# Four small reorderings around the end of the neighbour search in a four-layer graph kernel

## The reference

```python
z = _lap_mul(A, x) @ W1 + b1
z = jax.nn.leaky_relu(z, negative_slope=0.1)
d2 = sq[:, None] + sq[None, :] - 2.0 * (z @ z.T)
S = jnp.exp(-jnp.sqrt(jnp.maximum(d2, 0.0) + 1e-10) / 2.0)
S = jnp.where(ranks < 4, S, 0.0)          # the four nearest rows of each row
A2 = S + A
out = _lap_mul(A2, x) @ W2 + b2           # d * (A2 @ (d * x)), d from the row sums of A2
x = _layernorm(x + out)
...
h_N = jnp.matmul(adj, x)                  # fourth layer
out = jnp.maximum(concat([x, h_N]) @ W.T + b, 0.0)
```

## Time and profile before

| | us |
|---|---|
| median of three runs | 1466.86 |
| profiled execution, first to last instruction (span) | 1463.7 |
| PE busy | 1393.7 (95%) |
| DVE busy | 836.0 (57%) |
| ACT busy | 451.0 (31%) |
| POOL busy | 246.9 (17%) |

### The profile page before, as it was taken

One profiled execution on the slowest core, in us unless ns is written; L12 is line 12 of the kernel. 1 busy time (PEld: TensorE's weight loads), 2 busy tenths in 40 slices (PEclk: granted clock), 3 DMA queues, 4 the chain that ended last, 5 costly groups with the idle time before them and its releaser, 6 DMA issues.

```text
span 1463.7 us, 20350 instructions
## 1 busy us (share of the span) xinstructions
PE 1393.7 (95%) x7300; PEld 737.9 (50%) x7300; DVE 836.0 (57%) x1311; ACT 451.0 (31%) x979; POOL 246.9 (17%) x358
## 2 busy tenths in 40 slices
PE   6999999999999799999999987999999889999997
PEld 4776676666444354444544532444444344444454
DVE  6877766665224423323322269999999356555044
ACT  4776665665100000000000045666666200000011
POOL 2111110111100100000000000111111277774000
PEclk9999999999999999999999999999999989999999
DMA  9999998897998979788778520004443799999962
GB/s 311 400 383 389 365 331 300 325 318 266 359 382 331 379 308 346 306 316 328 298 292 310 227 72 1 15 17 137 134 130 115 242 370 401 380 386 394 352 234 71
DMA packets 112814, 403.26 MB, mean 276 GB/s; under 512 B 10368, under 2 KB 28384, under 8 KB 91232
## 3 DMA queue, kind: packets, MB, share of 16 engines
q1 hardware_dynamic: 72672, 314.33, 57.8%
q0 software_dynamic: 20576, 77.07, 14.0%
q10 hardware_dynamic: 19488, 10.80, 2.4%
HBM read 337.67 MB, written 64.49 MB: 275 GB/s over the span
## 4 chain that ended last, share of the span: by engine, by line
PE 70%; DVE 10%; DMA 10%; issue 7%; ACT 2%; POOL 0%; ACTq 0%; SPq 0%; DVEq 0%; POOLq 0%
PE acc L1137 10%; PE acc L1138 9%; PE acc L1139 9%; PE pt L1201 4%; DMA at_scratch<-region 3%; PE pt L1277 3%; PE pt L1278 3%; PE pt L1279 3%; DVE hT L1021 3%; PE pt L1137 3%; PE pt L1139 3%; PE pt L1138 3%; DMA region<-in_adj 3%; PE acc L1186 2%; PE acc L1182 2%
## 5 line engine op out<-in xcount | busy, mean ns | idle before, releaser
L1137 PE MATMUL acc<-region,yop 128*128 128x512 f16 x681 | 259.6, 381 | 16.6 <-DMA region<-at_scratch 16.6
L1201 PE MATMUL pt<-ident,region 128*128 128x128 f32 x1024 | 243.1, 277 | 18.8 <-DMA region<-in_adj 9.6
L1138 PE MATMUL acc<-region,yop 128*128 128x512 f16 x681 | 259.5, 381 | 0.0
L1139 PE MATMUL acc<-region,yop 128*128 128x512 f16 x681 | 259.5, 381 | 0.0
L969 DVE SCALAR_TENSOR_TENSOR region<-pt,region 128x512 f16<-128x512 f32 x200 | 135.3, 686 | 76.9 <-ACT region L631 76.4
L1201 PEld LDWEIGHTS pt<-ident,region 128*128 128x128 f32 x1024 | 145.9, 143 | 61.2 <-issue 16.1
L677 ACT ACTIVATE region<-pt 128x512 f32<-128x512 f32 x256 | 132.8, 602 | 109.4 <-PE pt L1284 95.8
L631 ACT ACTIVATE region<-pt 128x512 f16<-128x512 f32 x200 | 117.8, 596 | 108.6 <-PE pt L1201 94.0
L1021 DVE MAX8 hT<-region 128x8 f32<-128x4096 f32 x32 | 141.2, 4411 | 2.4 <-ACT region L677 2.4
L1137 PEld LDWEIGHTS acc<-region,yop 128*128 128x128 f16 x681 | 66.7, 98 | 98.7 <-issue 14.6
L598 ACT ACTIVATE std<-mv,eps_ln 128x4 f32<-128x4 f32 x32 | 9.5, 297 | 334.5 <-DVE mv L803 334.5
(11 more groups left out here) (235 smaller groups left out, 2157.8 us busy)
## 6 DMA issues: line engine op xcount, KB each, us to landing
region<-at_scratch SPq DMA_DIRECT2D x166, 1280.0 KB, 7.8
region<-in_adj SPq DMA_DIRECT2D x64, 1024.0 KB, 8.9
at_scratch<-region POOLq DMA_DIRECT2D x40, 768.0 KB, 7.0
at_scratch<-region POOLq DMA_DIRECT2D x40, 512.0 KB, 7.6
region<-at_scratch SPq DMA_DIRECT2D x76, 256.0 KB, 2.7
x_scratch<-xout ACTq DMA_DIRECT2D x16, 256.0 KB, 12.3
gath_all<-x_scratch POOLq DMA_DIRECT2D x12, 256.0 KB, 4.1
xin<-at_scratch SPq DMA_DIRECT2D x12, 256.0 KB, 2.8
```

Of the source, the lines that this page charges most:

```text
L1137: nc.tensor.matmul(into, y[:, 0, kt, :], high, start=(kt == first_tile), stop=False)
L1138: nc.tensor.matmul(into, y[:, 0, kt, :], low, start=False, stop=False)
L1139: return nc.tensor.matmul(into, y[:, 1, kt, :], high, start=False, stop=(kt == last_tile))
L1201: ins = nc.tensor.transpose(pt[kt % 4][:, t * P:(t + 1) * P], nat[u % 4][:, t, (kt % TPC) * P:(kt % TPC + 1) * P], ident[:, :])
```

## The change

Four things are moved; no arithmetic is added or removed.

1. PE: kept columns of chunks 4 and 5 no longer stand together ahead of row 24. The order is row 24, kept of chunk 4, projection of x2 of group 6, row 25, kept of chunk 5, turn of group 7, row 26, projection of group 7, rows 27 to 31.
2. POOL: the four residual loads are issued ahead of the small steps of group 7, behind the store of y of group 6.
3. ACT issues the late units 0, 1, 2 and 3; SP keeps the rest. Unit 0 waits for the search of row 30, units 1 and 2 for the search of row 31, unit 3 for y and its store.
4. The slot order of late units becomes 4, 3, 2, 1, 0 (it was 4, 3, 2, 0, 1).

```diff
-LATE_ORDER = [4, 3, 2, 0, 1]
+LATE_ORDER = [4, 3, 2, 1, 0]
-WIDE_REST = [24, 25, 26, 27, 28, 29, 30, 31]
-LATE_AT = {29: 0, 30: 1, 31: 2}
+ACT_LATE = 4
@@ sync
-                if kt in LATE_AT:
-                    sp.wait_ge(near_used, KT - 1 if LATE_AT[kt] == 0 else KT)
-                    load_late(LATE_AT[kt])
             sp.wait_ge(acc_full, nth(ALL, 4, WIDE - 1))
-            sp.wait_ge(yop_ready, nth(YOP, "y", NCH - 1))
-            sp.wait_ge(xT_full, nth(XT, 4, NCH - 1))
-            for b in range(2):
-                sp.wait_ge(y_stored[b], 16 * NCH // 2)
-            for k in range(len(LATE_AT), len(LATE)):
-                load_late(k)
+            for k in range(ACT_LATE, len(LATE)):
+                load_late(sp, k)
@@ gpsimd
+            def load_res():
+                pool.wait_ge(near_full, KT * NCH)
+                for t in range(TPC):
+                    pool.dma_start(res_rows(t // 2, 0, NCH)[:, :, t % 2, :], x2_rows[:, t, :, :]).then_inc(res_loaded, 16)
             for g in range(NCH):
+                if g == NCH - 1:
+                    load_res()
                 for stage_of in (distances, degree_sums, scales, low_y):
@@ scalar
             for i in range(KT + TPC + 1):
+                if i == KT:
+                    act.wait_ge(near_used, KT - 1)
+                    load_late(act, 0)
+                if i == KT + 1:
+                    act.wait_ge(near_used, KT)
+                    load_late(act, 1)
+                    load_late(act, 2)
...
+            act.wait_ge(yop_ready, nth(YOP, "y", NCH - 1))
+            act.wait_ge(xT_full, nth(XT, 4, NCH - 1))
+            for b in range(2):
+                act.wait_ge(y_stored[b], 16 * NCH // 2)
+            load_late(act, ACT_LATE - 1)
@@ tensor
+            wide_products(24)
+            kept_narrow(NARROW_KEPT[0])
+            pe.wait_ge(near_copied, copies(KT - 1, NCH - 1))
+            pe_project_x2(pe, NCH - 2)
+            wide_products(25)
+            kept_narrow(NARROW_KEPT[1])
+            pe_turn(pe, 4, NCH - 1)
+            wide_products(26)
+            pe_project_x2(pe, NCH - 1)
+            for kt in range(27, KT):
+                wide_products(kt)
```

More of the change, by code:

```diff
@@ L339, in load_x0, with load_late @@
             eng.dma_start(x0[:, part, :], x.rearrange("(t p) f -> p t f", p=P)[:, part, :]).then_inc(x0_loaded[q], 16)
+        def load_late(eng, k):
+            p, c, u = LATE[k]
+            slot = LATE_SLOTS[k]
+            if slot in LATE_SLOTS[:k]:
+                eng.wait_ge(*late_released(max(b for b in range(k) if LATE_SLOTS[b] == slot)))
+            eng.dma_start(ring[slot].rearrange("p k h n -> p (k h n)"), at_dram[c, u, :, :]
+                          ).then_inc(late_loaded_unit[slot], 16)
         block = ctx.enter_context(nc.Block())
@@ L406, in _ @@
             sp.wait_ge(acc_full, 4 * NCH)
[L407 to L413, removed]
             for kt in range(KEPT, KT):
@@ L537, in low_y @@
                                         ).then_inc(yop_ready, 1)
+            x2_rows = x_dram[2].rearrange("(c t p) f -> p t c f", p=P, t=TPC)
+            def load_res():
+                pool.wait_ge(near_full, KT * NCH)
+                for t in range(TPC):
+                    pool.dma_start(res_rows(t // 2, 0, NCH)[:, :, t % 2, :], x2_rows[:, t, :, :]).then_inc(res_loaded, 16)
             for g in range(NCH):
+                if g == NCH - 1:
+                    load_res()
                 for stage_of in (distances, degree_sums, scales, low_y):
@@ L547, in _ @@
                     load_x2(g + 2)
[L550 to L553, removed]
             pool.wait_ge(near_used, KT)
@@ L1377, in chunk_columns, with kept_narrow @@
                 return last
-            for c in NARROW_KEPT:
+            def kept_narrow(c):
                 pe.wait_ge(near_copied, copies(KT - 1, c))
                 chunk_columns(4, c, range(KEPT))
-                pe.wait_ge(near_copied, copies(KT - 1, NCH - 1))
-                if c == NARROW_KEPT[0]:
-                    pe_project_x2(pe, NCH - 2)
-                else:
-                    pe_turn(pe, 4, NCH - 1)
-            for kt in WIDE_REST:
+            wide_products(24)
[8 more added lines that the diff above has]
+            for kt in range(27, KT):
                 wide_products(kt)
-                if kt == WIDE_REST[1]:
-                    pe_project_x2(pe, NCH - 1)
             pe.wait_ge(near_copied, KT * NCH)
```

## The result

| | before | changed |
|---|---|---|
| median of four runs | 1466.98 us (1465.03 to 1467.61) | 1475.32 us (1474.55 to 1481.33) |
| ratio | | 1.0054, 95% interval 1.0033 to 1.0076 |
| span of the profiled execution | 1463.7 us | 1472.6 us |

The forecast was 1469.6 us, with a range of 1461 to 1474. The time fell outside it, on the slow side. A ratio of 1.0054 is 7.9 us; the interval goes from 4.8 to 11.2, so the change is clearly slower, if by little.

A forecast was written before the change was run, and what follows sets the result against it. The prediction took the chain from GpSimd's small steps through the gathers to VectorE's residuals as the limit. PE's projection of chunk 4 moves 1213.3 - 1210.56 = +2.7 us; 1463.7 + 2.7 + 3.2 = 1469.6 us, range 1461 to 1474.

The forecast's parts named there:

- the hold of the fourth load: On GpSimd, the fourth residual load waits for the three ahead, starting at 1162.4; distances start 16.7 us later.
- PE's wait for xT: Before the projection of group 7, PE, done with row 26 by 1153.5, waits for xT until 1168.
- end of the wide stage: PE finishes rows 28 to 31 at 1184 (1179 to 1187), against 1186.92 before.
- a wait of 4.0 for residual(0): At the projection of chunk 1, PE arrives at 1190.7 and waits 4 us for VectorE, until 1194.7.
- 1.7 for the clock: Between the projections of chunks 1 and 4, PE loses 1.7 us (0 to 2.3) at half clock after idling.
- 3.1 for the units: Two early ScalarE units, 2.62 MB, delay GpSimd's fourth load by 3.1 us, out of 0 to 7.4.
- a queue shares and doesn't block: On the DMA engines, GpSimd's and SyncE's queues took 61% and 41% when both had work.
- The units pass the loads: Rival, DMA engines from 1148: third load lands at 1166.3, gathers 1179.6; about +6 us, 1472.8; chance 15%.
- Held only until the first has landed: Rival, GpSimd's queue: the fourth load waits only for the first; gathers at 1168.5; -4.3 us, 1462.6; chance 21%.
- no hold: Rival, GpSimd's queue: the fourth load isn't held; distances at 1149.5, gathers at 1165.6; about -7 us, 1460; chance 11%.
- Faster by the whole 19 us: Rival, PE's rows 28 to 31: PE wins all 19 us; needs residual(0) by 1175; called excluded, no chance given.
- nothing gained, nothing lost: Late units issued by ScalarE: all but the last come earlier, with no gain or loss by itself.

The follow-up runs named there:

- e4: Changed kernel with late units issued by SyncE between tiles of rows 29 to 31 again (parts 3 and 4 undone): 1469.76 us, ratio 1.0006.
- e7: Changed kernel with PE's projection of group 7 moved behind row 27: 1476.27 us, ratio 1.0044 to the kernel before.
- e1: Changed kernel with the four residual loads put back behind GpSimd's small steps of group 7 (part 2 undone): 1470.62 us, ratio 1.0012 to before.
- e9: Changed kernel with each residual load cut into two of 256 KB, eight in all: 1474.92 us in a single run, no ratio.
- e2: Changed kernel with three residual loads early and only the fourth behind y's last store: 1466.83 us, ratio 0.9985 to the kernel before.
- e11: e2 with unit 3 issued by SyncE behind the wide rows instead of by ScalarE: 1462.75 us, ratio 0.9970 to the kernel before.
- e12: e11 with three small parameter loads of GpSimd, far ahead of the search, cut into eight: 1462.57 us, ratio 0.9962 to the kernel before.
- e8: Changed kernel with the four residual loads issued by ScalarE behind units 1 and 2 instead of by GpSimd: 1470.84 us, ratio 1.0008 to before.
- e10: Changed kernel with three small parameter loads of GpSimd, issued at 691 us, cut into eight: 1477.37 us, ratio 1.0066 to the kernel before.
- e6: Kernel before with part 2 alone (four residual loads ahead of the small steps of group 7): 1470.77 us, ratio 1.0012.

## Why the prediction was wrong

The chain up to the first gather went as forecast, only longer: the hold of the fourth load, the distances behind it, PE's wait for xT. The last part did not: PE's own wide stage, not its wait for VectorE, ended last. By the prediction's steps, measured times less the 1.95 us by which the search ended later:

| step | predicted | measured, less 1.95 |
|---|---|---|
| first load | 1145.9 | 1145.88 |
| fourth load | 1162.4 | 1164.91 |
| PE released by xT | 1168 | 1170.67 |
| y's last store issued | 1171.6 | 1174.23 |
| first gather | 1175.3 | 1178.68 |
| end of the wide stage | 1184 | 1193.73 |
| residual(0) ends | 1194.7 | 1197.89 |
| residual(3) ends | 1212.5 | 1216.76 |
| projection of chunk 4 | 1213.3 | 1217.36 |

The sum of the prediction went over PE: the end of the wide stage at 1184, 6.7 to the projection of chunk 1, a wait of 4.0 for residual(0), 16.9 to the projection of chunk 4, and 1.7 for the clock. Measured are 1193.73, 6.7, no wait, 16.9 and nothing for the clock. So the end of the wide stage was 9.7 us too early in it, and 5.7 us for a wait and a clock loss that did not come made up for more than half: that the sum was off by only 4.1 us (6.8 measured against 2.7) is in part luck. Two steps failed, the hold and the wide stage behind it.

**The step that failed first is the size of the hold.** The prediction put the fourth load 16.5 us after the first: 13.4 as before, and 3.1 for the units, out of a range of 0 to 7.4. It was 19.0. e4 shows that the base without units is 11.4, not 13.4, and the units' price 7.6: the upper end, not a value below the middle. Counted along VectorE's chain, which ended 0.6 us before PE's, that makes 2.5 of the 4.1 us by which the sum was too small. Another 0.9 came between the distances and the first gather (12.9 us and not 12.0; nearly all of it is y's last store), and 0.9 where residual(3) followed the first gather by 38.1 us and not 37.2; 0.2 goes the other way, as PE followed residual(3) by 0.6 us instead of 0.8. 2.5 + 0.9 + 0.9 - 0.2 = 4.1.

What made the choice of 3.1 wrong is in the queues' packets. In the earlier trace rows GpSimd's queue had 61% and SyncE's 41%, and from this the prediction read that a queue shares and doesn't block. That holds, but the share depends on the size of the pieces. The changed kernel with all three queues at work, from 1158 to 1162 (packets, MB, share of the 16 engines; q10 is ScalarE's, with the units):

```profile
q10 hardware_dynamic: 103, 0.94, 64.1%
q0 software_dynamic: 101, 0.36, 23.1%
q1 hardware_dynamic: 102, 0.21, 14.5%
```

and from the first load to the landing of the third, 1148 to 1167:

```profile
q10 hardware_dynamic: 288, 2.62, 38.1%
q1 hardware_dynamic: 1068, 1.93, 30.2%
q0 software_dynamic: 512, 1.84, 28.6%
```

103, 101 and 102 packets: each queue gets as many as the others, and the one with the large packets moves the most bytes. The Trainium skill (DMA: Bandwidth & Descriptors, "Queues, rings and completion order") says that each DMA engine serves its queues in turn, a packet at a time; the trace agrees, and so does that of before, with 356 packets of GpSimd's and 335 of SyncE's from 1160 to 1166. What was wrong is the 3 us that the prediction worked out from it. The units have 288 packets, and GpSimd's queue has 512 for y's store and three loads. With equal turns the units, begun from 1152 on, are all through before GpSimd's packets are: from 1164 to 1167 only 10 packets of the units are left, and 43 of GpSimd's. So all 2.62 MB go ahead of the end of the third load, which is the upper end of the range. One thing stays open here: from 1154 to 1158 SyncE's queue moved 13 packets, although tiles had been issued from 1152 on.

**A second step failed, on the path that ended last.** The end of the wide stage was put at 1184 and no later than 1187; it was 1193.73. Of the 9.7 us, 2.7 are the later xT. The rest is behind the wait: the prediction gave PE 16 us for the projection and rows 27 to 31, and it took 23.1 (1172.62 to 1195.68). 60 matmuls at 0.216 and the projection are 13.9 us; the lower clock cost 1.0 in the projection and 1.8 in the nine matmuls behind it; tiles were waited for 5.2 us; 1.2 us are in gaps that the profile does not put down to anything. The forecast had counted 1.7 for the clock, but at another place. It counted on the pace at which the tile buffers refill without giving the waits for tiles a term of their own. It also has PE waiting 4 us for residual(0); the trace shows VectorE waiting 0.33 us for PE. So the limit it named, VectorE's chain, was not the last one. But it was only 0.6 us ahead (residual(3)), and e7 shows it come out when PE's is shortened: ending the wide stage at 1184 would have gained 0.6 us at most. So neither chain can be named as the only one: with VectorE's as measured the projection of chunk 4 could have started at most 0.6 us earlier, and with PE's as measured not at all.

**The rivals.** "The units pass the loads", with 15%, is what happened on the DMA engines: the third load landed at 1166.5 (1164.5 by the clock of before; the rival had 1166.3, and put the point from which it decides at 1163). Its price of 6 us is near the 6.8 measured. Its way to it, a longer wait of PE for VectorE, was not. "Held only until the first has landed" and "no hold" are refuted by the eleven executions with four whole loads on GpSimd: in each the fourth began 0.3 to 0.4 us after the third had landed, and 4 to 10 us after the first had. "Faster by the whole 19 us" is refuted by e1, where PE had 6.7 us of it and lost them to residual(0).

**The step about the parts.** The prediction gave the ScalarE issues "nothing gained, nothing lost", and the price of the units to the hold. No part taken alone, and neither of two combinations, does harm that can be measured: part 1 +0.07%, part 2 +0.12%, 1 and 2 together (e4) +0.06%, 1 with 3 and 4 (e1) +0.12%. All together make +0.54%. With part 1 in place, the cost stands only where the units meet the loads while the small steps stand behind them. Parts 2, 3 and 4 without part 1 were not run, so whether the loss needs part 1 too is not shown.

**What stays open.** By which rule a queue gives room is not settled. Three whole loads or six halves go at once behind y's store, and e9's seventh half went 1.4 us later, when only that store had landed. "All ahead must be through" is also too strong for the fourth load. In e2, e11 and e12 a store of y stands between the third load and the fourth, and the fourth went 0.5 to 0.7 us before that store landed (e2: 1164.36 against 1156.48 + 8.5 = 1164.98). What it follows in all eleven executions is the landing of the third load. A larger queue for GpSimd would be the direct test; it wasn't tried. The drift of the search's end by up to 5.7 us between executions is not explained. And the timed loss of 7.9 us is 1.1 us above the 6.8 of the traced stretch, within the interval.

## What to carry to other kernels

A transfer that its queue can't take yet stops the engine that issues it, and everything behind it on that engine; put the one that won't fit behind the work that others wait for (e2: one instruction moved, from +0.54% to -0.15%). Its length is set by what all queues have outstanding. Here the queues got equal numbers of packets, so count packets: a queue that has fewer and larger ones left than yours gets all its bytes through before you are done. Sum all their bytes as the upper end, and stay near it in that case. Where two chains end within a us of each other, as here PE's wide rows and VectorE's gathers, an edit has to move both, and the forecast needs both worked out to the same care.

## What the runs showed of the hardware that I had not expected

ScalarE's queue stops its engine too: 14.65 us in four loads of 512 KB behind two units of 1280 KB (e8), while the two units themselves took 0.9 us to issue. Three queues at work got the same number of packets, 103, 101 and 102 in 4 us, with packets of 9.1, 3.6 and 2.1 KB on average, and so 64%, 23% and 15% of the engines. Room went by amount: three loads of 512 KB or six of 256 KB at once behind a store of 256 KB (e9), with no effect of five small transfers more before (e10). And the fourth load followed the third's landing by about 0.4 us, whether it started 9.3 us (e6), 11.4 (e4) or 19.0 (the changed kernel) after the first.
